# One-hot tables of a MoE dispatch with the column innermost, in 16-bit operands; the column numbers on VectorE; the first block's rows on their own semaphore

## What is computed

```python
for j in range(2):                                   # layer 0: 6 experts, top 2, and 2 shared units
    gate = xf @ router_W[j] + router_b[j]
    _, ids = top_k(gate + gate_bias[j], 2)
    weights = softmax(where(sel(ids), gate, -inf))
    combined = einsum('ne,enh->nh', weights, experts(xf))
    xf = rmsnorm(xf + combined + shared(xf)) * norm_w[j]
...
gate_scores, expert_idx = top_k(tokens @ gate_w.T, 2)   # layer 1: 8 experts, top 2
combine = zeros((T, 8)).at[arange(T)[:, None], expert_idx].add(softmax(gate_scores))
out = sum over experts e of combine[:, e] * (gelu(tokens @ W1[e].T + B1[e]) @ W2[e].T + B2[e])
```

## Time and profile before

| | us |
|---|---|
| median of 3 runs | 1994.8 (1993.05 to 1995.58) |
| the profiled execution | 1997.71 |
| its span | 1995.9 |
| PE busy in the span | 1758.9 (88%) |
| DVE, ACT, POOL busy | 1408.3, 1030.8, 819.1 |

### The profile page before, as it was taken

One profiled execution on the slowest core, in us unless ns is written; L12 is line 12 of the kernel. 1 busy time (PEld: TensorE's weight loads), 2 busy tenths in 40 slices (PEclk: granted clock), 3 DMA queues, 4 the chain that ended last, 5 costly groups with the idle time before them and its releaser, 6 DMA issues.

```text
span 1995.9 us, 31811 instructions
## 1 busy us (share of the span) xinstructions
PE 1758.9 (88%) x11154; PEld 1554.7 (78%) x11154; DVE 1408.3 (71%) x2519; ACT 1030.8 (52%) x2084; POOL 819.1 (41%) x868
## 2 busy tenths in 40 slices
PE   5899999999999989999959899998489982999990
PEld 4788888888888878888858788887266782999990
DVE  4665465556444988777757977776799787788876
ACT  4344334334422434655555355553697462888882
POOL 2132232232222115777721257776221041788840
PEclk9899999999998999999979899999699985999995
DMA  4100000000012332666654136664700023788858
GB/s 158 64 1 11 11 9 1 11 11 0 11 57 96 112 108 61 207 194 204 181 174 139 60 115 192 197 197 144 234 32 1 1 72 119 230 275 277 264 178 263
DMA packets 147066, 233.01 MB, mean 117 GB/s; under 512 B 28163, under 2 KB 103173, under 8 KB 141957
## 3 DMA queue, kind: packets, MB, share of 16 engines
q1 hardware_dynamic: 123332, 167.04, 25.7%
q0 software_dynamic: 23616, 64.52, 10.7%
HBM read 175.65 MB, written 55.33 MB: 116 GB/s over the span
## 4 chain that ended last, share of the span: by engine, by line
PE 64%; issue 13%; DVE 12%; POOL 5%; ACT 3%; DMA 2%; POOLq 0%; SPq 0%; DVEq 0%; ACTq 0%
PE bank L171 44%; PE bank L2113 4%; PE bank L1287 3%; PE bank L421 2%; PE bank L1296 1%; PE bank L439 1%; POOL a_aTm L909 1%; PE bank L2528 1%; POOL a_xa L894 1%; PE bank L1211 1%; POOL a_rs L163 1%; DVE d_back L2678 1%; PE bank L228 1%; PE bank L2338 1%; PE bank L1346 1%
## 5 line engine op out<-in xcount | busy, mean ns | idle before, releaser
L182 POOL TENSOR_TENSOR spare_g<-neg_half 128x1 f32<-128x1 f32 x80 | 20.2, 253 | 594.5 <-ACT a_sg L552 142.4
L171 PE MATMUL bank<-gT_hi,w_hi 128*128 128x512 f32 x592 | 245.8, 415 | 0.0
L171 PE MATMUL bank<-gT_hi,w_lo 128*128 128x512 f32 x592 | 237.0, 400 | 0.0
L171 PE MATMUL bank<-gT_lo,w_hi 128*128 128x512 f32 x592 | 235.7, 398 | 0.0
L1816 POOL DMA_INDIRECT got<-b_rows,b_gather_i x168 | 170.7, 1016 | 67.3 <-issue 50.6
L1606 DVE TENSOR_TENSOR gT_lo<-bank,gT_hi 128x512 fp32r<-128x512 f32 x148 | 97.0, 690 | 134.0 <-ACT gT_hi L1429 103.6
L1459 ACT ACTIVATE m_hi<-gs 128x512 fp32r<-128x512 f32 x116 | 72.9, 633 | 124.3 <-DVE gs L1613 67.6
L171 PE MATMUL bank<-w_hi,m_hi 128*128 128x256 f32 x464 | 131.8, 284 | 5.2 <-DVE sent L1635 5.2
L171 PEld LDWEIGHTS bank<-gT_hi,w_lo 128*128 128x128 f32 x592 | 113.0, 191 | 27.4
L171 PE MATMUL bank<-w_lo,m_hi 128*128 128x256 f32 x464 | 131.7, 284 | 0.0
L171 PE MATMUL bank<-w_hi,m_lo 128*128 128x256 f32 x464 | 131.5, 283 | 0.0
(11 more groups left out here) (455 smaller groups left out, 5738.1 us busy)
## 6 DMA issues: line engine op xcount, KB each, us to landing
v_raw<-in_units SPq DMA_DIRECT2D x39, 1024.0 KB, 5.0
w_raw<-in_units SPq DMA_DIRECT2D x56, 256.0 KB, 4.4
shared<-in_units SPq DMA_DIRECT2D x40, 256.0 KB, 3.1
b_rows<-x SPq DMA_DIRECT2D x16, 512.0 KB, 3.1
got<-b_rows SPq DMA_DIRECT2D x16, 512.0 KB, 4.5
close_back<-b_kept SPq DMA_DIRECT2D x16, 512.0 KB, 7.9
d_back<-d_kept SPq DMA_DIRECT2D x16, 512.0 KB, 8.7
w_raw<-b_folded SPq DMA_DIRECT2D x26, 256.0 KB
```

What stands on the lines that cost most here:

```text
L171: ins = pe.matmul(out, a, b, start=first and n == 0, stop=last and n == of - 1)
```

## The change

1. The three one-hot tables change their layout: the 16 columns of a part become the innermost index. `hot_in` is [partition, part, 128, 16] instead of [partition, column, 128], likewise `hot_at` and `hot_id`. PE reads one column of such a table, so its weights and moving values lie 16 elements of 2 bytes apart, a step of 32 bytes, instead of side by side.
2. The numbers compared are 16-bit: `in_h` and `at_h` in bf16 instead of `in_f` and `at_f`, and new constant tables `iota_h`, `iotaq_h` (each value four times, HOT_RUN) and `turn_h`, cast once from the f32 ones.
3. The multiply by column numbers is on DVE for all columns of all dispatches; POOL's in the first MoE and ACT's in the second are gone.
4. In the second MoE the first block's two gathers signal a semaphore of their own, for which turn(0) waits; turn(1) waits for the other two.

```diff
@@ inverse, first MoE (PE) @@
-            ins = pe.matmul(B[6][:, 0:2 * NQB], b.hot_in[:, col, :], b.hot_id[:, col, :, :].rearrange("p a q -> p (a q)"), start=col == 0, stop=col == COLS // 4 - 1)
+            ins = pe.matmul(B[6][:, 0:2 * NQB], b.hot_in[:, 0, :, col], b.hot_id[:, 0, :, :, col].rearrange("p a q -> p (a q)"), start=col == 0, stop=col == COLS // 4 - 1)
@@ tables (DVE) @@
     v.tensor_copy(b.every, b.ones[:, :]).then_inc(link.sem, 1)
     v.wait_ge(link.sem, link.next())
+    v.tensor_copy(b.iota_h, spread(b.disp[:, DISP["iota"]], HOT_RUN)).then_inc(link.sem, 1)
+    v.wait_ge(link.sem, link.next())
+    v.tensor_copy(b.iotaq_h, spread(b.disp[:, DISP["iotaq"]], HOT_RUN)).then_inc(link.sem, 1)
+    v.wait_ge(link.sem, link.next())
+    v.tensor_copy(b.turn_h, b.disp[:, DISP["turn"]]).then_inc(link.sem, 1)
+    v.wait_ge(link.sem, link.next())
@@ hot_vector (DVE) @@
-    v.tensor_tensor(b.hot_at[:, :, :], mid(b.disp[:, DISP["iotaq"]][:, 0:NQB], COLS // 4), spread(b.at_f[:, cs], NQB), ALU.is_equal).then_inc(r.hot_at.sem, 1)
-    v.tensor_tensor(b.hot_in[:, :, :], mid(b.disp[:, DISP["iota"]], COLS // 4), spread(b.in_f[:, cs], P), ALU.is_equal).then_inc(r.hot_in.sem, 1)
+    v.tensor_tensor(by_run(b.hot_at[:, 0]), hot_runs(b.iotaq_h[:, 0:NQB, :]), hot_cols(b.at_h[:, cs], NQB), ALU.is_equal).then_inc(r.hot_at.sem, 1)
+    v.tensor_tensor(by_run(b.hot_in[:, 0]), hot_runs(b.iota_h), hot_cols(b.in_h[:, cs], P), ALU.is_equal).then_inc(r.hot_in.sem, 1)
+    v.wait_ge(r.hot_at.sem, r.hot_at.at(4 * rnd + j))
+    v.tensor_tensor(b.hot_id[:, 0, 0], b.hot_at[:, 0], mid(b.turn_h[:, cs], NQB), ALU.mult).then_inc(r.hot_turn.sem, 1)
@@ b_gpsimd (POOL) @@
-        g.tensor_tensor(b.hot_id[:, :, 0, :], b.hot_at[:, :, :], spread(b.disp[:, DISP["turn"]][:, cs], NQB), ALU.mult).then_inc(r.hot_turn.sem, 1)
@@ dispatch_vector (DVE); its two tables change as in hot_vector @@
-        v.tensor_tensor(b.hot_id[:, mine, 0, :], b.hot_at[:, mine, :], spread(table("turn")[:, mine], nq), ALU.mult).then_inc(r.hot_turn.sem, 1)
+        v.tensor_tensor(b.hot_id[:, j, 0], b.hot_at[:, j], mid(b.turn_h[:, cs], nq), ALU.mult).then_inc(r.hot_turn.sem, 1)
@@ dispatch_scalar (ACT) @@
-        for col in range(cs.start + TURN_COLS, cs.stop):
-            act.activation(b.hot_id[:, col, 0, :], b.hot_at[:, col, :], ACT.Copy, scale=float(col))
...
@@ gathers in d_gpsimd (POOL) and turn in d_tensor (PE) @@
+            landed = r.first_rows if q < QBD else r.gathered[n % 6]
...
+        if k == 0:
+            pe.wait_ge(r.first_rows.sem, r.first_rows.at(0))
+        else:
+            pe.wait_ge(r.gathered[n % 6].sem, r.gathered[n % 6].at(n // 6, 16 * gathers_of(n)))
```

More of the change, by code:

```diff
@@ L39 @@
 FOLD_GAP = 544
-TURN_COLS = 8
+HOT_RUN, HOT_COLS = 4, PICKS * N // P // 4
 BACKS = 3
@@ L207, with by_run @@
 LATE_BANKS = (4, 5, 6, 7, 0)
+def hot_runs(table):
+    return table.unsqueeze(2).broadcast_to([P, table.shape[1], HOT_COLS // HOT_RUN, HOT_RUN])
+def hot_cols(values, n):
+    return values.rearrange("p (a b) -> p a b", b=HOT_RUN).unsqueeze(1).broadcast_to([P, n, HOT_COLS // HOT_RUN, HOT_RUN])
+def by_run(tab):
+    return tab.rearrange("p n (a b) -> p n a b", b=HOT_RUN)
 def modulation_scalar(act, b, s):
@@ L1462, in hot_part @@
         act.wait_ge(r.hot_at.sem, r.hot_at.at(4 * rnd + j))
-        act.activation(b.hot_id[:, :, 1, :], b.hot_at[:, :, :], ACT.Copy, scale=b.disp[:, DISP["p1"]]).then_inc(r.hot_part.sem, 1)
+        act.activation(b.hot_id[:, 0, 1], b.hot_at[:, 0], ACT.Copy, scale=b.disp[:, DISP["p1"]]).then_inc(r.hot_part.sem, 1)
     for j, now, after, third in turn_steps(rnd):
@@ L1764, in places_vector @@
     v.wait_ge(link.sem, link.next())
-    v.tensor_copy(b.in_f, b.in_i).then_inc(link.sem, 1)
+    v.tensor_copy(b.in_h, b.in_i).then_inc(link.sem, 1)
     v.wait_ge(link.sem, link.next())
-    v.tensor_copy(b.at_f, b.at_i).then_inc(link.sem, 1)
+    v.tensor_copy(b.at_h, b.at_i).then_inc(link.sem, 1)
     v.wait_ge(link.sem, link.next())
@@ L1802, in b_gpsimd @@
 def b_gpsimd(g, b, s, r, dram, rnd):
-    def hot(j):
-        cs = slice(j * COLS // 4, (j + 1) * COLS // 4)
-        g.wait_ge(r.hot_at.sem, r.hot_at.at(4 * rnd + j))
-        g.tensor_tensor(b.hot_id[:, :, 0, :], b.hot_at[:, :, :], spread(b.disp[:, DISP["turn"]][:, cs], NQB), ALU.mult).then_inc(r.hot_turn.sem, 1)
     def gathers(k):
@@ L1829, in b_gpsimd @@
             prep_rs_gpsimd(g, b, r, t)
-    for j in range(4):
-        hot(j)
     g.wait_ge(r.gather_at.sem, r.gather_at.at(rnd))
@@ L2401, in dispatch_vector @@
         cs = slice(j * COLS // 4, (j + 1) * COLS // 4)
-        mine = slice(cs.start, cs.start + TURN_COLS)
-        v.tensor_tensor(b.hot_at[:, cs, :], mid(table("iotaq")[:, 0:nq], COLS // 4), spread(b.at_f[:, cs], nq), ALU.is_equal).then_inc(r.hot_at.sem, 1)
-        v.tensor_tensor(b.hot_in[:, cs, :], mid(table("iota"), COLS // 4), spread(b.in_f[:, cs], P), ALU.is_equal).then_inc(r.hot_in.sem, 1)
+        v.tensor_tensor(by_run(b.hot_at[:, j]), hot_runs(b.iotaq_h[:, 0:nq, :]), hot_cols(b.at_h[:, cs], nq), ALU.is_equal).then_inc(r.hot_at.sem, 1)
+        v.tensor_tensor(by_run(b.hot_in[:, j]), hot_runs(b.iota_h), hot_cols(b.in_h[:, cs], P), ALU.is_equal).then_inc(r.hot_in.sem, 1)
         v.wait_ge(r.hot_at.sem, r.hot_at.at(j))
-        v.tensor_tensor(b.hot_id[:, mine, 0, :], b.hot_at[:, mine, :], spread(table("turn")[:, mine], nq), ALU.mult).then_inc(r.hot_turn.sem, 1)
+        v.tensor_tensor(b.hot_id[:, j, 0], b.hot_at[:, j], mid(b.turn_h[:, cs], nq), ALU.mult).then_inc(r.hot_turn.sem, 1)
     v.wait_ge(r.inverse.sem, r.inverse.at(0))
@@ L2429, in dispatch_tensor @@
         pe.wait_ge(r.hot_part.sem, r.hot_part.at(j))
-        for col in range(j * COLS // 4, (j + 1) * COLS // 4):
-            ins = pe.matmul(b.bank[2][:, 0:2 * nq], b.hot_in[:, col, :], b.hot_id[:, col, :, :].rearrange("p a q -> p (a q)"), start=col == 0, stop=col == COLS - 1)
+        for col in range(HOT_COLS):
+            ins = pe.matmul(b.bank[2][:, 0:2 * nq], b.hot_in[:, j, :, col], b.hot_id[:, j, :, :, col].rearrange("p a q -> p (a q)"),
+                            start=j == 0 and col == 0, stop=j == 3 and col == HOT_COLS - 1)
     ins.then_inc(r.inverse.sem, 1)
@@ L2436, in dispatch_scalar @@
     for j in range(4):
-        cs = slice(j * COLS // 4, (j + 1) * COLS // 4)
         act.wait_ge(r.hot_at.sem, r.hot_at.at(j))
-        for col in range(cs.start + TURN_COLS, cs.stop):
-            act.activation(b.hot_id[:, col, 0, :], b.hot_at[:, col, :], ACT.Copy, scale=float(col))
-        act.activation(b.hot_id[:, cs, 1, :], b.hot_at[:, cs, :], ACT.Copy, scale=b.disp[:, DISP["p1"]]).then_inc(r.hot_part.sem, 1)
+        act.activation(b.hot_id[:, j, 1], b.hot_at[:, j], ACT.Copy, scale=b.disp[:, DISP["p1"]]).then_inc(r.hot_part.sem, 1)
 W1, W2 = KD * HID, KH * D
@@ L2483, in gathers @@
             q = n * GROUP * QBD + c
-            g.indirect_dma_start(b.got[n % 6][:, c, :], None, rows, bass.IndirectOffsetOnAxis(b.gather_i[:, q:q + 1], 0)).then_inc(r.gathered[n % 6].sem, 16)
+            landed = r.first_rows if q < QBD else r.gathered[n % 6]
+            g.indirect_dma_start(b.got[n % 6][:, c, :], None, rows, bass.IndirectOffsetOnAxis(b.gather_i[:, q:q + 1], 0)).then_inc(landed.sem, 16)
     def scatters(k):
@@ L2521, in turn @@
         n, at = k // GROUP, (k % GROUP) * QBD
-        pe.wait_ge(r.gathered[n % 6].sem, r.gathered[n % 6].at(n // 6, 16 * gathers_of(n)))
+        if k == 0:
+            pe.wait_ge(r.first_rows.sem, r.first_rows.at(0))
+        else:
+            pe.wait_ge(r.gathered[n % 6].sem, r.gathered[n % 6].at(n // 6, 16 * gathers_of(n)))
         if k >= 2:
@@ L2774, in program @@
         b.disp = sb(after_a, "disp", [P, NDISP])
+        b.iota_h, b.iotaq_h = sb(after_a, "iota_h", [P, P, HOT_RUN], BF16), sb(after_a, "iotaq_h", [P, NQ, HOT_RUN], BF16)
+        b.turn_h = sb(after_a, "turn_h", [P, COLS], BF16)
         b.before, b.every = sb(after_a, "before", [P, P], BF16), sb(after_a, "every", [P, P], BF16)
@@ L2790, in dispatch_buffers, with hot_buffers @@
             b.where = sb(scope, n + "where", [P, E, NT])
-            b.slot_f, b.in_f, b.at_f = (sb(scope, n + what, [P, COLS]) for what in ("slot_f", "in_f", "at_f"))
+            b.slot_f = sb(scope, n + "slot_f", [P, COLS])
+            b.in_h, b.at_h = (sb(scope, n + what, [P, COLS], BF16) for what in ("in_h", "at_h"))
             b.slot_i, b.in_i, b.at_i = (sb(scope, n + what, [P, COLS], I32) for what in ("slot_i", "in_i", "at_i"))
             b.found, b.source, b.padding = (sb(scope, n + what, [P, w]) for what, w in (("found", 2 * nq), ("source", nq), ("padding", nq)))
-        def hot_buffers(scope, name, nq, cols):
-            b.hot_in, b.hot_at = sb(scope, name + "_hot_in", [P, cols, P], BF16), sb(scope, name + "_hot_at", [P, cols, nq], BF16)
-            b.hot_id = sb(scope, name + "_hot_id", [P, cols, 2, nq], BF16)
+        def hot_buffers(scope, name, nq, parts):
```

(9 more changed lines are left out.)

## The result

The changed kernel takes 2030.76 us (median of 4 runs, 2029.83 to 2034.34) against 1995.19: a ratio of 1.0173, with a 95% interval from 1.0158 to 1.0187. It is slower, the way that was forecast, but by 35.6 us where 16.5 were forecast, and above the range's end of 2017.

What follows compares the result with a forecast made beforehand. PE was taken to bound the kernel (64% of the span): rounds' first parts -1.6 and -2.5, six later parts +21.0, second MoE +0.55, first rows -2.0, tables +1.05, together +16.5 on 1994.8 gives 2011 us; range 1978 to 2017.

Steps and rivals of the forecast that it cites:

- C: The forecast, all twelve parts' matmuls: PE pays 1.74 ns per column for the 32-byte step; 2008 to 2016 us, chance 0.50.
- the later parts: Parts 2 to 4 of both first-MoE rounds, PE their only limit: 4.68 us each instead of 1.17, +21.0 for six.
- price per column: PE's stepped read in the one-hot matmuls: 1.74 ns per column, so 292 ns for 168 columns, 4.68 us a part.
- a lower clock after the slow parts: PE's gates behind slow parts: adds up to 2.5 us, from round 1's gate of 4.26 instead of 2.84; outside the sum.
- round 0's first part: First MoE: PE starts at 732.56 instead of 735.96 and the gate ends at 740.1 against 741.70, -1.6 us.
- The casts' wait: Three casts of constant tables in DVE's queue ahead of PE's gate at 680.04: +1.05 us.
- The gain of the first rows: Second MoE's first block: turn(0) waits for two gathers instead of four, up(0) at 1697.2 instead of 1699.23, -2.0 us.
- DVE's pace: DVE's table operations with two 16-bit sources: 0.53 ns per element instead of 1.04; hot_in 1.245 us, column numbers 0.87.
- Rival B: Half pace on PE: 143 ns per matmul, 2.29 us a part; -9.5, 1985 us, chance 0.20.
- A: Rival: PE reads the 32-byte step at today's pace; -16.2, 1979 us, chance 0.18.
- D: Rival: weights and columns share PE's read, 515 ns a matmul, 8.24 us a part; 2054 us, chance 0.07.
- E: Rival: DVE gets no faster on 16-bit operands; -1, 1994 us if PE reads freely, chance 0.05.

## Why the prediction was wrong

- **The likeliest case was the right one, C.** PE pays for the stepped read, the later parts show it, and the second MoE turns from DVE's pace to PE's: its 64 matmuls now lie on the chain in one piece.

```profile
1704.51 18.66 PE bank L2445 x64
```

- **The price per column was 6% low.** I took 1.74 ns from DVE's row L2383; the matmuls show 5.00 / 16 / 168 = 1.86, 1.81 of it the moving read and the rest the weights'. The prediction had the better row itself, PE's own 512 four-byte columns in 232 ns, 16 bytes per 1.81 ns, and named it as an upper end. The engine's own densest stream was the limit; that DVE's row came so near is luck as far as the runs show, none of which ties the two engines' reads together. Cost: 22.9 instead of 21.0 us in the later parts, and 18.66 instead of 17.4 in the second MoE.
- **The step that failed is the clock.** The prediction wrote that "a lower clock after the slow parts" adds "up to 2.5", taken from one gate of 4.26 instead of 2.84, and left it out of the sum. In the sum every gate stood at 2.84. One gate like that costs 1.4, so 2.5 does not cover two; there are seven behind slow parts besides the first of round 1, and the six later ones alone cost 7.9. In round 0's first part the gate at 3.93 costs 1.1 and eats most of the gain of 1.6. The casts' wait came out as forecast, 1.0 for 1.05, but the gate behind it ran at the lower clock and added 1.6. Together that is 7.9 + 1.1 + 1.6, over half of the 20 us by which the forecast missed.
- **The gain of the first rows** was counted as kept. It is there at the first block, -2.2, about as forecast, and by the thirteenth block it is lost, with 1.1 us more; in the waits it goes where PE and DVE wait behind POOL's queue. The prediction priced what is late next for the first block, not for the blocks behind it.
- **DVE's pace** was right: 1218 ns forecast as 1245, 858 as 870. The Trainium skill, "VectorE: DVE Perf Modes", section "The perf-mode tier table", has 1224 ns for this shape; the trace now agrees.
- **The rule weighed against the change.** The Trainium skill, "Advanced Engine Details and Errata", section "SBUF Cachelines", speaks of 16-byte lines and of two hits on a line that absorb the latency. The 16 bytes agree with the runs: the price stops growing there. The two hits don't, for PE's moving read: at 8 bytes a line is hit twice, and the matmul takes 154 ns instead of 77. Rival B, read out of that sentence, would have given 2.29 us a part at 32 bytes; it was 5.00.
- **Rivals A, D and E fall**: A and E by the parts' 5.00 us and hot_in's 1218 ns, D by the run with only the weights stepped.

What stays open: which of the gates falls to the lower clock, and why the first rows end at +1.2 us in the changed kernel, at nothing in the one with the step of 4 bytes and at -0.8 and -0.9 with steps of 8 and 16.

## What to carry to other kernels

A layout that makes one engine fast is paid by every engine that reads it: look first at who reads the table and at what step, and price that engine's stream by its own densest row. Two columns innermost were enough for DVE's fast pace and left PE's reads at a step of 4 bytes, and with the casts off the path that version takes 1978.45 us against 1996.18 of the kernel before, measured beside it. And where PE is made to wait or to crawl, count the lower clock once for every place where it can follow, not once in all.

## What the runs showed of the hardware that was not expected

- PE's moving read goes as if by 16-byte pieces at about 1.8 ns each: 77, 154, 307 and 304 ns for 168 two-byte columns at steps of 4, 8, 16 and 32 bytes (the last with the weights near). At the lower clock the price in time is the same: the second MoE's matmuls of 156 columns took 18.66 / 64 = 292 ns, 1.87 a column, at a granted clock of 0.50, and the part at 751.22 us took 1.86 a column at 1.00.
- Weights at a 32-byte step cost 7 ns a matmul (84 against 77), though each load is recorded at 147 ns instead of 97.
- PE at work on stepped reads is busy in the rows of the profile, and still the granted clock fell behind it, to 0.51 to 0.64 in the gates behind the six later parts: in 5 of 6 cases of the changed kernel and of that with the step of 16 bytes, in 6 of 6 with the old DVE code, in 3 of 6 with the moving table alone at 32 bytes, and in none with steps of 4 and 8 bytes.
- DVE keeps its fast pace with runs of only two neighbouring 16-bit values: hot_in took 1218 ns with runs of 2 as with runs of 4.
